# Layer 3 of a graph network: GpSimd waits for every tenth gather to land, and the edge products are planned later and further apart

## The chip, the cores and the metric

One core of one Trainium2 chip runs the whole program in one launch. The metric is the device time of that launch in microseconds (us). The kernel before takes 5139.83 us, the median of three runs that lie between 5138.98 and 5140.54. The profile is one more execution, which took 5172.93 us with the profiler on; its instructions span 5171.2 us of that.

## The reference, cut to what matters

Four layers of a graph network are applied one after another to 6250 nodes with 128 features and 100,000 directed edges, sorted by destination. Only the last one, layer 3, is touched. It is ten steps of a propagation (APPNP):

```
src, dst = edges plus one loop for each node
norm     = 1/sqrt(deg[src]) * 1/sqrt(deg[dst])
xk = h
for step in range(10):
    agg = segment_sum(norm[:, None] * xk[src], dst)      # for each node, over its edges
    xk  = 0.9 * agg + 0.1 * h
out = x + relu(xk)
```

Each step needs the whole result of the step before it.

## The kernel before, in words

The nodes lie in 49 tiles of 128. In layer 3 the sum over edges is done in two ways.

**Dense part.** For the destination tiles 0 to 39 (`DENSE` = 40) the kernel has built a dense matrix of edge counts in fp8, which is read from HBM again in every step. TensorE takes these tiles in ten chunks of four. A chunk is 49 source tiles times 2 matmuls (a high and a low fp16 half of the node values), 98 matmuls of 128x512, all into one PSUM bank (line 1952). ScalarE copies the bank out (line 1438), TensorE turns it back with four transposes (line 1964), and VectorE combines it with the residual (line 2849); ScalarE (line 1429) and VectorE (line 2827) make the two fp16 halves for the next step.

**Edge part.** For the other nine tiles, 40 to 48 (the "pooled" tiles), the sum goes over edges. Their edges fill 145 tiles of 128. GpSimd gathers the 128 source rows of each with an indirect DMA from HBM (line 1003), from `table` in one step and from `x_spill` in the next. VectorE makes a one-hot matrix of destinations (line 2837, "hots"), and TensorE multiplies the two (line 1982). Four edge tiles are one group (`EG`), so a step has 37 groups, the last of one tile. The gathered rows go to a ring of five groups (`ERING`): GpSimd waits on `edge_used` until the group five before has been multiplied. The one-hots have a ring of four (`EHOT`). Before a step's first gather GpSimd waits on `y_out`, which counts the stores of the whole result of the step before to HBM (SyncE, line 762).

**The order.** Every engine of layer 3 goes through one and the same list, `plan`. An entry has a due time in units of one dense matmul. A step is `LONG` = 980 units (10 chunks of 98). A chunk's copy is due at its end, its turn ten units later (`TURN_LAG`) and its store 26 units later (`STORE_LAG`), so those of the last chunk fall into the next step. The products of edge group g are due at `EDGE_LAG + EDGE_GAP * g` = 64 + 20 g units of their step, the last group at 784; the one-hots of a group come 50 units ahead of it. A pooled tile is finished with its last group, and its store comes 16 units later. The sort puts these entries between the dense matmuls; the engines then run their lists in order and wait on semaphores, so TensorE stands still if a group's rows have not landed. SyncE's list holds the stores and the loads of the dense matrix. GpSimd does not follow the plan: it runs through the gathers as fast as the rings let it.

`tiles_done(step, i)` gives the number of finished node tiles, in the plan's order, up to tile i of a step. In step 1 and later, the dense matmuls of chunk 0 wait at source tiles 0, 32, 36 and 48 until the step before has finished what they read (`READ_UPTO`).

Of the kernel before, what the change touches and what calls it, by code (L numbers as in the profile page):

```python
# [15 lines left out]
P = 128  # L16
N_NODES, N_EDGES, D = 6250, 100000, 128
# [27 lines left out]
AS_KEPT_FIRST = 4  # L45
ADJ_PITCH = 1 << 13
CHUNKS = (DENSE + CHUNK - 1) // CHUNK
TURN_LAG, STORE_LAG, EDGE_LAG, EDGE_GAP = 10, 26, 64, 20
SCALE = 1024.0

BD, BK = 5, 26
# [37 lines left out]
def build(nc, t, out):  # L89
    ctx = ExitStack()  # L90
    with ctx:
# [262 lines left out]
            return (near_last[i] - edge_first) // EG  # L354

        LONG = chunk_at_cost(CHUNKS)
        finished = [(chunk_at_cost(c + 1) + TURN_LAG, list(chunk_nodes(c))) for c in range(CHUNKS)]
        finished += [(EDGE_LAG + EDGE_GAP * pooled_group(i), [i]) for i in range(DENSE, NT)]
        done_order = [i for _, some in sorted(finished) for i in some]
        place = {i: p for p, i in enumerate(done_order)}  # L360
        STORES = CHUNKS + POOLED

        plan = []
        for step in range(STEPS):
            base = step * LONG
            for c in range(CHUNKS):
                for i in range(NT):
                    plan.append((base + chunk_at_cost(c) + 2 * i * len(chunk_nodes(c)) / CHUNK, 0, "dense", step, c, i))
                plan.append((base + chunk_at_cost(c + 1), -1, "copy", step, c, 0))
                plan.append((base + chunk_at_cost(c + 1) + TURN_LAG, 1, "turn", step, c, 0))  # L370
                plan.append((base + chunk_at_cost(c + 1) + STORE_LAG, 4, "store", step, c * CHUNK, chunk_nodes(c).stop))
            for g in range(EGROUPS):
                plan.append((base + EDGE_LAG + EDGE_GAP * g, 2, "edges", step, g, 0))
                plan.append((base + EDGE_LAG + EDGE_GAP * g - 5 * EDGE_GAP // 2, 5, "hots", step, g, 0))
            for i in range(DENSE, NT):
                plan.append((base + EDGE_LAG + EDGE_GAP * pooled_group(i), 3, "pooled", step, i, 0))
                plan.append((base + EDGE_LAG + EDGE_GAP * pooled_group(i) + STORE_LAG - TURN_LAG, 4, "store", step, i, i + 1))
        plan = [entry[2:] for entry in sorted(plan, key=lambda entry: entry[:2])]

        def tiles_done(step, i):  # L380
            return step * NT + place[i] + 1

        READ_UPTO = {0: 32, 32: 36, 36: NT - 1, NT - 1: NT}

# [464 lines left out]
        def _(pool):  # L849
# [141 lines left out]
            def after_l2(b):  # L991
                if b == 0:
                    pool.sem_inc(sem("edge_used"), ERING - AS_KEPT_FIRST)
                    def two_steps(pairs):
                        for half in range(2):
                            pool.wait_ge(sem(f"y_out{half}"), pairs * (16 * STORES) + (16 * STORES if half else 16 * PTN))
                            settle(pool)
                            for g in range(EGROUPS):
                                pool.wait_ge(sem("edge_used"), pairs * (2 * EGROUPS) + (half * EGROUPS + g + 1))
                                settle(pool)  # L1000
                                for k in range(group_size(g)):
                                    tile = edge_first + g * EG + k
                                    pool.indirect_dma_start(  # L1003
                                        out=y_rows[:, g % ERING, k, :], out_offset=None, in_=(table, x_spill)[half],
                                        in_offset=bass.IndirectOffsetOnAxis(ap=src_i[:, tile:tile + 1], axis=0)
                                    ).then_inc(y_in[g % ERING], 16)

                    for pairs in range(STEPS // 2 - 1):
                        two_steps(pairs)
                    two_steps(STEPS // 2 - 1)  # L1010
                if b:
                    with pool.Fori(0, STEPS) as s:
                        pool.wait_ge(sem("y_stored"), s * 16 + 16)
                        settle(pool)
                        sweep(s + 3, table, src_i)
                        wait_runs(s + 4)
                        node_rows(runs, nodes(Db), sem("nodes3"))
# [503 lines left out]
        def _(pe):  # L1521
# [363 lines left out]
            def after_l2(b):  # L1885
# [46 lines left out]
                if b == 0:  # L1932
# [4 lines left out]
                    for kind, step, what, i in plan:  # L1937
                        n = step * CHUNKS + what
                        if kind == "dense":
                            some, y = chunk_nodes(what), halves((E, A)[step % 2])  # L1940
                            r = [i < last for _, last in PARTS3].index(True)
                            piece, at = n * len(PARTS3) + r, (i - PARTS3[r][0]) * P
                            if i == PARTS3[r][0]:
                                pe.wait_ge(sem(f"adj_in{piece % ADJ_RING}"), 16 * (piece // ADJ_RING + 1))
                            if i == 0 and n >= 2:
                                pe.wait_ge(sem("turn_in"), n - 1)
                            if n == 0 and i % T7 == 0:
                                pe.wait_ge(sem("y_lower0"), i // T7 + 1)
                            if n > 0 and what == 0 and i in READ_UPTO:
                                pe.wait_ge(sem("lower"), max(tiles_done(step, j) for j in range(READ_UPTO[i])))  # L1950
                            for h in range(2):
                                mm = pe.matmul(chunk_banks[n % 2][:, 0:len(some) * P], y[:, i, h * D:(h + 1) * D],  # L1952
                                               adj_ring[:, piece % ADJ_RING, 0:len(some), at:at + P],
                                               start=(i == 0 and h == 0), stop=(i == NT - 1 and h == 1))
                            if i == NT - 1:
                                mm.then_inc(sem("chunk_made"), 1)
                            elif i + 1 == PARTS3[r][1]:
                                mm.then_inc(sem("piece_used"), 1)
# [8 lines left out]
                        if kind == "edges":  # L1967
                            g, r = what, what % ERING
                            pe.wait_ge(y_in[r], step * row_loads[r] + y_in_before[r]
                                       + 16 * sum(group_size(q) for q in range(r, g + 1, ERING)))  # L1970
                            pe.wait_ge(sem("edge_hot_made"), step * EGROUPS + g + 1)
                            for k in range(group_size(g)):
                                tile = edge_first + g * EG + k
                                of = [i for i in near(tile) if i >= DENSE]
                                for i in of:
                                    first = max(near_first[i], edge_first)
                                    if tile == first:
                                        if i - 2 >= DENSE:
                                            tiles_free(step, i - 2)
                                        else:  # L1980
                                            tiles_free(step - 1, max(range(DENSE + (i - DENSE) % 2, NT, 2)))
                                    mm = pe.matmul(edge_banks[i % 2][:, 0:2 * D], step_hot[g % EHOT][:, k, i % 2 * P:(i % 2 + 1) * P],  # L1982
                                                   y_rows[:, r, k, :].bitcast(F16),
                                                   start=(tile == first), stop=(tile == near_last[i]))
                                    if tile == near_last[i]:
                                        mm.then_inc(sem("multiplied"), 1)
                            if g < EGROUPS - 1:
                                mm.then_inc(sem("edge_used"), 1)
# [77 lines left out]
        def _(dve):  # L2066
# [658 lines left out]
            def after_l2(b):  # L2725
# [81 lines left out]
                if b == 0:  # L2807
# [22 lines left out]
                    for kind, step, what, _ in plan:  # L2830
                        if kind == "hots":
                            g, nth = what, step * EGROUPS + what
                            if nth >= EHOT:
                                dve.wait_ge(sem("edge_used"), ERING + nth - EHOT + 1)
                            for k in range(group_size(g)):
                                at = edge_first + g * EG + k
                                a = dve.tensor_scalar(step_hot[g % EHOT][:, k, :], iota_y, dst_f[:, at:at + 1], UNIT,
                                                      ALU.is_equal, MUL)
                            a.then_inc(sem("edge_hot_made"), 1)
                        if kind == "turn":  # L2840
# [217 lines left out]
```

## Time and profile before

| what | value |
| --- | --- |
| median of 3 runs | 5139.83 us |
| profiled execution | 5172.93 us |
| its span | 5171.2 us |
| PE busy in the span | 4366.7 us, 84% |
| GpSimd (POOL) busy | 3123.1 us, 60% |
| layer 3, first to last dense matmul start | 2726.2 to 5160.7 us |
| gathers of layer 3 (line 1003) | 1450, mean 954 ns |
| idle time of GpSimd before them | 588.3 + 516.2 us |

Layer 3 is the second half of the span, about 2435 us in ten steps. In the 40 slices of the profile the digits of PE are all 9 there, and those of GpSimd are 4 to 7. The profiled execution is some 33 us longer than the median of the unprofiled ones.

### The profile page before, as it was taken

What the parts mean: (1) busy time and instruction counts of PE and PEld (TensorE: products, weight loads), DVE (VectorE), ACT (ScalarE), POOL (GpSimd) and SP (SyncE); (2) the same over time, 40 slices, a digit from 0 to 9 for tenths busy, and PEclk for the clock granted to TensorE, in tenths of its full rate; (3) what the DMA queues carried; (4) which work ended last, traced back from release to release, by engine and by line L of the source; (5) the groups of instructions that cost most, each with busy time, mean ns of one, the idle gap of its engine ahead of it and who ended that gap; (6) DMA issues with size and microseconds to landing.
All of it is one profiled execution on the core that took longest, in us unless ns stands there. A gap on an engine that the chain in (4) does not pass through costs nothing.

```text
span 5171.2 us, 68624 instructions
## 1 busy us (share of the span) xinstructions
PE 4366.7 (84%) x24174; PEld 2788.4 (54%) x24174; DVE 2619.2 (51%) x8500; ACT 1031.3 (20%) x2920; POOL 3123.1 (60%) x3205
## 2 busy tenths in 40 slices
PE   3798589999984556566668999999999999999999
PEld 3676466666664555555544444444454545454444
DVE  7898545665554677777884222323232323222232
ACT  5787411111111011112241000000000000000001
POOL 2554277777776777777725564747474747465564
PEclk9999789999996676787688999999999999999999
DMA  5322222222222333333316565656565656565564
GB/s 149 96 101 92 85 67 71 70 66 71 70 70 74 96 95 97 95 94 95 87 31 194 186 188 178 196 182 190 182 192 181 193 181 188 182 192 185 184 191 144
DMA packets 454493, 682.92 MB, mean 132 GB/s; under 512 B 89793, under 2 KB 235879, under 8 KB 454128
## 3 DMA queue, kind: packets, MB, share of 16 engines
q1 hardware_dynamic: 346116, 463.55, 28.6%
q0 software_dynamic: 101664, 211.69, 15.7%
q8 instruction: 198, 3.24, 0.3%
q10 hardware_dynamic: 6364, 3.20, 0.2%
q14 instruction: 151, 1.24, 0.1%
HBM read 595.40 MB, written 83.11 MB: 131 GB/s over the span
## 4 chain that ended last, share of the span: by engine, by line
PE 30%; POOL 18%; issue 7%; DVE 6%; DMA 4%; ACT 1%; POOLq 0%; DVEq 0%
PE ps L1952 23%; POOL arena L1003 13%; POOL E L968 5%; PE pt L1982 2%; DMA arena<-table,src_i 2%; PE ps L1774 2%; DVE B L2481 1%; DMA arena<-x_spill,src_i 1%; DVE arena L2523 1%; PE pt L1791 1%; PE pt L1782 1%; PE ps L1964 1%; DMA E<-gat_table,src_i 0%; PE ps L1901 0%; ACT C L1303 0%
## 5 line engine op out<-in xcount | busy, mean ns | idle before, releaser
L1952 PE MATMUL ps<-arena,E 128*128 128x512 fp8e4 x4900 | 1099.8, 380 | 7.0 <-DVE C L2750 7.0
L1952 PE MATMUL ps<-arena,A 128*128 128x512 fp8e4 x4900 | 1095.7, 379 | 0.0
L1003 POOL DMA_INDIRECT arena<-table,src_i x725 | 691.8, 954 | 588.3 <-DMA table<-E 368.9
L1003 POOL DMA_INDIRECT arena<-x_spill,src_i x725 | 691.5, 954 | 516.2 <-DMA x_spill<-A 296.8
L953 POOL DMA_INDIRECT arena<-table,src_i x782 | 741.8, 949 | 355.2 <-issue 235.9
L968 POOL DMA_INDIRECT E<-gat_table,src_i x782 | 762.5, 975 | 270.7 <-issue 234.1
L1697 PE MATMUL ps<-E,arena 128*128 128x352 f32 (+22 forms) x2932 | 740.5, 404 | 113.8 <-DMA arena<-table,src_i 112.8
L1952 PEld LDWEIGHTS ps<-arena,E 128*128 128x128 f16 x4900 | 480.5, 98 | 539.6 <-DVE C L2750 7.2
L1952 PEld LDWEIGHTS ps<-arena,A 128*128 128x128 f16 x4900 | 479.4, 98 | 529.1
L1697 PEld LDWEIGHTS ps<-E,arena 128*128 128x128 f32 x2932 | 493.5, 202 | 287.4 <-DMA arena<-table,src_i 136.0
L2849 DVE SCALAR_TENSOR_TENSOR C<-ps,sc_b,scores 128x128 f32<-128x128 f32 x400 | 112.6, 344 | 821.7 <-PE ps L1964 820.6
L2401 DVE SCALAR_TENSOR_TENSOR E<-arena,pt 128x512 f32<-128x512 bf16 (+5 forms) x782 | 478.5, 674 | 24.7 <-PE ps L1697 23.9
L1774 PE MATMUL ps<-arena,B 128*128 128x144 f32 x2244 | 475.1, 362 | 0.0
L1774 PEld LDWEIGHTS ps<-arena,B 128*128 128x128 f32 x2244 | 389.5, 239 | 8.1 <-issue 6.0
L1038 POOL DMA_INDIRECT A<-first_rows,src_i x145 | 213.5, 1472 | 210.6 <-PE pt L2020 117.2
L2862 DVE SCALAR_TENSOR_TENSOR scores<-pt,sc_b,scores 128x128 f32<-128x128 f32 x90 | 31.6, 351 | 597.4 <-PE pt L1982 597.0
L1822 PE MATMUL pt<-ident,E 128*128 128x128 f32 x56 | 25.3, 452 | 360.3 <-ACT E L1237 360.3
L1507 ACT ACTIVATE E<-ps 128x490 fp8e4<-128x490 f32 (+1 forms) x520 | 307.2, 596 | 92.2 <-PE ps L2036 88.2
L2045 PE MATMUL pt<-arena,E 128*128 128x258 f16 x1960 | 305.0, 276 | 1.0 <-ACT E L1507 1.0
L1438 ACT ACTIVATE O<-ps 128x512 f32<-128x512 f32 x100 | 59.7, 597 | 1118.7 <-PE ps L1952 1118.4
L2977 DVE TENSOR_SCALAR O<-arena 128x245 bf16<-128x245 bf16 x1040 | 232.3, 278 | 37.4 <-PE ps L2036 37.2
L2481 DVE TENSOR_SCALAR B<-w_gat,dst_f 128x256 f32<-128x256 bf16 x784 | 245.0, 381 | 0.0
(351 smaller groups left out, 4748.5 us busy)
## 6 DMA issues: line engine op xcount, KB each, us to landing
arena<-adj SPq DMA_DIRECT2D x200, 1024.0 KB
arena<-adj SPq DMA_DIRECT2D x100, 1088.0 KB
adj<-E SPq DMA_DIRECT2D x40, 784.0 KB, 3.4
O<-dst_rows SPq DMA_DIRECT2D x112, 224.0 KB, 3.5
arena<-table,src_i POOLq DMA_INDIRECT x1507
x_spill<-A SPq DMA_DIRECT2D x50, 256.0 KB
E<-gat_table,src_i POOLq DMA_INDIRECT x782
E<-in_etype SPq DMA_DIRECT2D x781, 16.0 KB
```

The source lines that it names most:

```text
L953: pool.indirect_dma_start(out=rows_ring[:, k % RING, :], out_offset=None, in_=table, in_offset=bass.IndirectOffsetOnAxis(ap=src_i[:, k:k + ...
L968: pool.indirect_dma_start(out=att_rows[:, b % 3 * AB + at, :], out_offset=None, in_=gat_table, in_offset=bass.IndirectOffsetOnAxis(ap=src_ ...
L1003: pool.indirect_dma_start(out=y_rows[:, g % ERING, k, :], out_offset=None, in_=(table, x_spill)[half], in_offset=bass.IndirectOffsetOnAxis ...
L1038: pool.indirect_dma_start(out=rows0[:, x % (2 * EG0), :], out_offset=None, in_=first_rows, in_offset=bass.IndirectOffsetOnAxis(ap=src_i[:, ...
L1507: act.activation(made[:, i % MADE, :, 2 * BD * q:2 * BD * q + w], ps[pair % 4][:, 0:w * NT].rearrange("p (d j) -> p j d", j=NT), ACT.Copy, ...
L1697: mm = pe.matmul(ps[m % 4][:, (lo - WD * m) * BASES:(hi - WD * m) * BASES], rows_ring[:, k % RING, :], m_ring[:, k % MS, lo - first_dst(k) ...
L1774: mm = pe.matmul(ps[i % 2][:, 0:WL2], edge_hot[:, (2 * b + half) % 3, k % AH, i % 2 * P:(i % 2 + 1) * P], weighted_rows[:, b % 2, k, :], s ...
L1952: mm = pe.matmul(chunk_banks[n % 2][:, 0:len(some) * P], y[:, i, h * D:(h + 1) * D], adj_ring[:, piece % ADJ_RING, 0:len(some), at:at + P] ...
L2045: mm = pe.matmul(bank0_of(m)[:, 0:2 * LO], made[:, m % MADE, j, :], y16[:, j, :], start=(j == 0), stop=(j == NT - 1))
L2401: dve.scalar_tensor_tensor(m_ring[:, k % MS, w, :], bc(iota_h[:, w], BASES), dst_rel[:, k:k + 1], row_bc(made_c[:, c % 2, at, :], w.stop - ...
L2481: a = dve.tensor_scalar(edge_hot[:, g % 3, k, :], iota_y, dst_f[:, g * AH + k:g * AH + k + 1], None, ALU.is_equal)
L2977: dve.tensor_scalar(hot_code[:, g % HOT, 0:BW], iota_w[:, 0:BW], slot_c[:, g // P, g % P:g % P + 1], None, ALU.is_equal).then_inc(sem("hot ...
```

## The change

GpSimd gets a wait behind every tenth gather of a step, counted from the step's start (14 waits in the 145 gathers of a step): until that gather has landed. The edge groups are planned at 84 + 25 g instead of 64 + 20 g units of a step, and at 148 + 25 g in the first step. With this the last group is due at 984 units, four units into the next step, and in the first step at 1048, 68 units into the second. As tiles of one step now finish while the next one runs, the finishing order is read off the plan for all steps at once instead of being computed for one step, and the ring of one-hots is counted through all steps, not anew in each.

```diff
-TURN_LAG, STORE_LAG, EDGE_LAG, EDGE_GAP = 10, 26, 64, 20
+TURN_LAG, STORE_LAG, EDGE_LAG, EDGE_LATE, EDGE_GAP = 10, 26, 84, 148, 25
...
-        finished = [(chunk_at_cost(c + 1) + TURN_LAG, list(chunk_nodes(c))) for c in range(CHUNKS)]
-        finished += [(EDGE_LAG + EDGE_GAP * pooled_group(i), [i]) for i in range(DENSE, NT)]
-        done_order = [i for _, some in sorted(finished) for i in some]
-        place = {i: p for p, i in enumerate(done_order)}
...
+            first = base + (EDGE_LAG if step else EDGE_LATE)
             for g in range(EGROUPS):
-                plan.append((base + EDGE_LAG + EDGE_GAP * g, 2, "edges", step, g, 0))
-                plan.append((base + EDGE_LAG + EDGE_GAP * g - 5 * EDGE_GAP // 2, 5, "hots", step, g, 0))
+                plan.append((first + EDGE_GAP * g, 2, "edges", step, g, 0))
+                plan.append((first + EDGE_GAP * g - 5 * EDGE_GAP // 2, 5, "hots", step, g, 0))
...
+        done = [(step, i) for kind, step, what, _ in plan if kind in ("turn", "pooled")
+                for i in (chunk_nodes(what) if kind == "turn" else [what])]
+        place = {of: p for p, of in enumerate(done)}
...
         def tiles_done(step, i):
-            return step * NT + place[i] + 1
+            return place[step, i] + 1
...
                                     ).then_inc(y_in[g % ERING], 16)
+                                    if (g * EG + k) % 10 == 10 - 1:
+                                        pool.wait_ge(y_in[g % ERING], y_in_before[g % ERING]
+                                                     + (2 * pairs + half) * row_loads[g % ERING] + 16 * (k + 1)
+                                                     + 16 * sum(group_size(q) for q in range(g % ERING, g, ERING)))
...
-                                    mm = pe.matmul(edge_banks[i % 2][:, 0:2 * D], step_hot[g % EHOT][:, k, ...],
+                                    mm = pe.matmul(edge_banks[i % 2][:, 0:2 * D], step_hot[(step * EGROUPS + g) % EHOT][:, k, ...],
```

## Rows read from the trace of the kernel before

**Rows 1.** The head of the page: the span, and TensorE's busy time in it.
```profile
span 5171.2 us, 68624 instructions
PE 4366.7 (84%) x24174; PEld 2788.4 (54%) x24174; DVE 2619.2 (51%) x8500; ACT 1031.3 (20%) x2920; POOL 3123.1 (60%) x3205
```

**Rows 2.** Waits of TensorE in layer 3: us in total, times, longest.
```profile
PE pt L1982 <- DMA arena<-table,src_i: 33.4, 28, 15.6
PE pt L1982 <- DMA arena<-x_spill,src_i: 19.8, 25, 1.7
```

**Rows 3.** Stretches: length, PE busy (instructions), granted clock, DMA share, GB/s.
```profile
2726.00:2987.00 261.00, 241.50 (x1205) 0.96 0.60 189
2987.00:3229.50 242.50, 237.40 (x1211) 1.00 0.59 186
```

**Rows 4.** The dense line: durations in ns, first and last start in us.
```profile
L1952 PE MATMUL ps<-arena,E x4900: 378/379/634, 2726.2 to 4919.9; 128*128 128x512 fp8e4 x196
L1952 PE MATMUL ps<-arena,A x4900: 379/379/380, 2987.1 to 5160.7; 128*128 128x512 fp8e4 x196
```

**Rows 5.** Pieces of the chain of waits: start, us, what.
```profile
2902.93 7.05 DMA arena<-table,src_i
...
2947.16 21.15 PE ps L1952 x98
...
3237.23 0.73 issue
...
3306.57 0.44 PE ps L1964 x4
...
3317.17 0.44 PE pt L1982 x4
```

**Rows 6.** Timeline, third step: start, us, engine, line [idle before <-releaser].
```profile
3237.96 0.94 POOL L1003 DMA_INDIRECT arena<-table,src_i  x1 [60.32 <-DMA table<-E]
...
3244.23 0.61 PE L1982 MATMUL pt<-arena,rows 128*128 128x256 f16 x4
...
3250.21 0.61 PE L1982 MATMUL pt<-arena,rows 128*128 128x256 f16 x4 [1.06 <-DMA arena<-table,src_i]
...
3260.72 0.61 PE L1982 MATMUL pt<-arena,weight_e 128*128 128x256 f16 x4 [0.40 <-DMA arena<-table,src_i]
...
3276.12 0.61 PE L1982 MATMUL pt<-arena,rel_i 128*128 128x256 f16 x4 [0.31 <-DMA arena<-table,src_i]
...
3418.76 0.95 POOL L1003 DMA_INDIRECT arena<-table,src_i  x1 [0.30 <-issue]
```

**Rows 7.** Timeline, first step, its first gather and first edge group.
```profile
2726.18 17.30 PE L1952 MATMUL ps<-arena,E 128*128 128x512 fp8e4 x66 [7.00 <-DVE C L2750]
...
2752.80 0.94 POOL L1003 DMA_INDIRECT arena<-table,src_i  x1 [130.41 <-DMA table<-E]
...
2759.04 1.04 PE L1982 MATMUL pt<-arena,rows 128*128 128x256 f16 x4 [15.57 <-DMA arena<-table,src_i]
2759.87 5.91 PE L1952 MATMUL ps<-arena,E 128*128 128x512 fp8e4 x20
```

**Rows 8.** Stretch behind the 7 us idle time, columns as in Rows 3.
```profile
2726.00:2731.00 5.00, 4.82 (x12) 0.50 1.04 392
```

**Rows 9.** Timeline: end of a step's pooled work, and a last chunk's store.
```profile
3234.78 0.36 SPq L762 DMA_DIRECT2D table<-E  x1
...
3427.26 0.27 PE L1982 MATMUL pt<-arena,rows 128*128 128x256 f16 x1
...
3429.10 3.45 SPq L762 DMA_DIRECT2D x_spill<-A  x2
...
3432.08 1.13 DVE L2817 SCALAR_TENSOR_TENSOR scores<-C,sc_a,B 128x128 f32<-128x128 f32 x4
```

**Rows 10.** Timeline, the end of the last step.
```profile
5162.52 1.12 DVE L2849 SCALAR_TENSOR_TENSOR C<-ps,sc_b,scores 128x128 f32<-128x128 f32 x4 [16.87 <-PE ps L1964]
```

**Rows 11.** DMA of the third step, 3189 to 3430 us: packets, MB, share.
```profile
q0 software_dynamic: 4640, 9.51, 13.9%
```

More of the change, by code:

```diff
@@ L371, in build @@
                 plan.append((base + chunk_at_cost(c + 1) + STORE_LAG, 4, "store", step, c * CHUNK, chunk_nodes(c).stop))
+            first = base + (EDGE_LAG if step else EDGE_LATE)
             for g in range(EGROUPS):
-                plan.append((base + EDGE_LAG + EDGE_GAP * g, 2, "edges", step, g, 0))
-                plan.append((base + EDGE_LAG + EDGE_GAP * g - 5 * EDGE_GAP // 2, 5, "hots", step, g, 0))
+                plan.append((first + EDGE_GAP * g, 2, "edges", step, g, 0))
+                plan.append((first + EDGE_GAP * g - 5 * EDGE_GAP // 2, 5, "hots", step, g, 0))
             for i in range(DENSE, NT):
-                plan.append((base + EDGE_LAG + EDGE_GAP * pooled_group(i), 3, "pooled", step, i, 0))
-                plan.append((base + EDGE_LAG + EDGE_GAP * pooled_group(i) + STORE_LAG - TURN_LAG, 4, "store", step, i, i + 1))
+                plan.append((first + EDGE_GAP * pooled_group(i), 3, "pooled", step, i, 0))
+                plan.append((first + EDGE_GAP * pooled_group(i) + STORE_LAG - TURN_LAG, 4, "store", step, i, i + 1))
         plan = [entry[2:] for entry in sorted(plan, key=lambda entry: entry[:2])]
+        done = [(step, i) for kind, step, what, _ in plan if kind in ("turn", "pooled")
+                for i in (chunk_nodes(what) if kind == "turn" else [what])]
+        assert [step for step, _ in done] == [step for step in range(STEPS) for _ in range(NT)]
+        place = {of: p for p, of in enumerate(done)}
         def tiles_done(step, i):
-            return step * NT + place[i] + 1
+            return place[step, i] + 1
         READ_UPTO = {0: 32, 32: 36, 36: NT - 1, NT - 1: NT}
@@ L1949, in after_l2 @@
                             if n > 0 and what == 0 and i in READ_UPTO:
-                                pe.wait_ge(sem("lower"), max(tiles_done(step, j) for j in range(READ_UPTO[i])))
+                                pe.wait_ge(sem("lower"), max(NT + tiles_done(step - 1, j) for j in range(READ_UPTO[i])))
                             for h in range(2):
@@ L1981, in after_l2 @@
                                             tiles_free(step - 1, max(range(DENSE + (i - DENSE) % 2, NT, 2)))
-                                    mm = pe.matmul(edge_banks[i % 2][:, 0:2 * D], step_hot[g % EHOT][:, k, i % 2 * P:(i % 2 + 1) * P],
+                                    mm = pe.matmul(edge_banks[i % 2][:, 0:2 * D], step_hot[(step * EGROUPS + g) % EHOT][:, k, i % 2 * P:(i % 2 + 1) * P],
                                                    y_rows[:, r, k, :].bitcast(F16),
@@ L2836, in after_l2 @@
                                 at = edge_first + g * EG + k
-                                a = dve.tensor_scalar(step_hot[g % EHOT][:, k, :], iota_y, dst_f[:, at:at + 1], UNIT,
+                                a = dve.tensor_scalar(step_hot[nth % EHOT][:, k, :], iota_y, dst_f[:, at:at + 1], UNIT,
                                                       ALU.is_equal, MUL)
```

## The prediction

> **What bounds the kernel now.** I read the head of the page first: the span is 5171.2 us and PE is busy for 84% of it [rows 1]. The dense line of layer 3 starts at 2726.2 us and its last matmul at 5160.7 us [rows 4], so the ten steps take 2434.7 us; nothing ahead of them is touched. The stretches of the first two steps, cut at the first dense matmul of each, are 261 and 242.5 us long with PE busy for all but a few us in the second [rows 3]. Steps 2 to 10 together are (5160.9 - 2987.1), which is 241.5 us each [rows 4]. The bound is TensorE, and what it waits for inside layer 3 is the landing of gathers: 33.4 us and 19.8 us, of which one wait is 15.6 us [rows 2].
>
> What would a step take without waits? In the chain 98 dense matmuls take 21.15 us, 215.8 ns each, a chunk's four transposes 0.44 us, four edge matmuls 0.44 us [rows 5]. The second step has 1211 matmuls [rows 3], 980 dense, 40 transposes, and about 189 of edges. So 980 x 0.2158 = 211.5, plus 10 x 0.44 = 4.4, plus 189 x 0.11 = 20.6: **236.5 us**. A later step loses 241.5 - 236.5 = 5.0 us, nine of them 45 us. This is more than the waits say (37.6 us), since a wait also costs the drain and refill around it; I take the difference of lengths. The first step loses 24.4 us. Of these about 4.3 belong to its start: 66 dense matmuls took 17.30 us [rows 7] instead of 14.2, behind a 7 us idle time, and some waiting for the state. The other 20.1 are the edges: 15.57 us of waiting for the first group and, behind it, 20 dense matmuls in 5.91 us [rows 7] instead of 4.48. So **65 us hang on late gathers**, and this is all that the change can win.
>
> Why are they late? In the third step GpSimd issues its first gather at 3237.96 and its 145th at 3418.76 [rows 6]: 180.8 us over 144 gaps, 1.256 us a gather, 5.02 us for four. TensorE asks for a group every 20 units: 20 x 0.2158 + 20.6/37 + a share of the transposes 0.09 = 4.96 us. The two have the same pace, the gathers a little slower. TensorE reaches its first group just when it lands and then has no lead, so that each gather with a longer latency stops it.
>
> **The new plan.** At 25 units a group TensorE asks every 25 x 0.2158 + 0.56 + 0.11 = 6.06 us, and its first group comes 20 units = 4.3 us later. Without the new wait GpSimd would gain a us on every group and soon be held by the ring of five. No stall of a step would be left except at its start. The number of edge matmuls is unchanged.
>
> **The new wait.** The profile before has no such wait; the price is worked out from landings. Gather n of the third step starts at 3237.96 + 1.256 n. The first group's last gather (n = 3) starts at 3241.7 and TensorE goes on at 3244.23: 2.5 us. The other groups of the first eight for which it waited give 3.5 (n = 7, 3250.21), 4.0 (n = 15, 3260.72) and 4.4 us (n = 27, 3276.12) [rows 6]; the four without a wait landed sooner than asked for. The longest piece of the chain from a gather's issue to its landing that I use is 7.05 us [rows 5]. TensorE meets the late ones, so a typical landing is nearer to the first two: 3.4 us. GpSimd then resumes; behind the y_out wait this took 0.73 us [rows 5], with more than one wait in it; I take 0.4. A wait puts off the next gather, which would have come 1.256 us after the tenth, by 3.4 + 0.4 - 1.26 = **2.6 us** (bounds: 1.3 from the fastest landing and an instant restart, 6.5 from the longest and 0.73). 14 waits are 36 us a step, and GpSimd's pace becomes 5.02 + 36/36.25 = 6.0 us a group, again the same as TensorE's 6.06. Behind the waiting instruction stand only the next gathers; their cover is the lead.
>
> How long is the cover? The step of rows 6 began at 3229.5 [rows 3], so its gathers started 8.5 us into it. In the changed kernel VectorE does the last pooled tile first, about 0.8 us in the way of the last chunk, which makes it 9.3. The last gather then lands at 9.3 + 180.8 + 36 + 3.4 = 229.5; TensorE wants the last group at 236.5 + 4 units = 237.4. The slack is 8 us, or 0.55 us for each wait. **A wait may cost 3.15 us before a step becomes longer.** At the start the lead is 84 x 0.2158 + 0.44 = 18.6 against a first landing at 9.3 + 3.8 + 2.5 to 3.5, two to three us. I leave 3 us in all for single late landings in the eight later steps.
>
> The Trainium skill ("DMA: Bandwidth & Descriptors", section "Anatomy of one DMA — SWDGE (gpsimd) path") fits a DMA as 2.0 us plus its bytes over 436 GB/s. A gather here is 9.51 MB/145 = 66 KB [rows 11], so it says 2.15 us, an estimate from that page. The fastest landing read above is 2.5 us and the others up to 4.4, so the trace is above the rule; by it a wait would cost 1.3 us and the sum below would be some 4 us better.
>
> **The first two steps.** The first gather of layer 3 starts at 2752.80 [rows 7], set by the stores ahead of it, 26.6 us into the step. Group 0 is now wanted at 148 units, 31.9 + 0.4 + the slow start 3.1 = 35.4 us, 2761.6; it landed at 2759.04. The 15.57 us and the slower stretch behind them go. They are partly paid in the second step: the last group of the first is due 68 units into it, 14.7 + 0.44 + 1.0 = 16.1 us. From such a last group to its store are 3429.10 - 3427.26 = 1.84 us, and from a store to the first gather 3237.96 - 3234.78 = 3.18 us [rows 6, 9]. So gathers start at 21.1 us, group 0 lands at 21.1 + 3.8 + 3 = 27.9, and TensorE wants it at 18.1 + 0.44 + 1.0 = 19.6: a stall of **8.3 us**. Behind 7 us of idle time the clock was 0.50, the 1.2 GHz level, for 5 us [rows 8], twelve matmuls where 23 fit: I add **3 us**. From there the pace is even, and the third step starts as usual.
>
> Chunk 0 of the second step reads tile 48 at unit 96, 28 units (6 us) behind the last group; 1.84 us are enough. SyncE's stores move with their tiles; the ones past which a step's gathers wait is the last chunk's (unit 1006), behind tile 48's (unit 1000), in all steps but the first.
>
> **The end.** Group 36, its VectorE work of some 1.5 us and four residual operations of 1.13 us [rows 9] now stand ahead of the last chunk's, which began 1.6 us behind the last dense matmul [rows 4, 10]: about **1.5 us**.
>
> **Sum.** 65 - 8.3 - 3 - 3 - 1.5 = 49 us. The profiled execution would go from 5172.9 to 5124. Profiled and unprofiled differ by 33 us of which I cannot place any, so I take the same 49 us off the median: 5139.8 - 49 = **5091 us**.
>
> **Rivals.** *A wait of no weight.* If landings are near the 2.5 us row, or the restart instant, the 3 us and a us of the second step's stall go: 5086. For it speaks the first group; against it the three longer ones.
>
> *The gathers become the pace.* If a wait costs 3.3 us, in the middle between mine and the rows of late landings, nine steps grow by 14 x (3.3 - 3.15) + about a us for uneven landings, 3 us each: 5118. For it: the two paces, 6.0 and 6.06, are a tie.
>
> *The gathers overrun the step (the other side).* The place is GpSimd's queue: each us over 3.15 a wait costs 14 us a step, 140 in all, so from 3.5 us a wait (a mean landing of 4.35 with my restart) the gain is gone. At a mean landing of 5 us, as the chain's longer pieces, a wait costs 4.15: 140 us more, 5231. For it: the dense matrix is loaded beside the gathers at 186 GB/s [rows 3], and landings of 7.05 us exist. Against it: 317 of 370 groups were never waited for (53 waits [rows 2]) though GpSimd was no faster than TensorE.
>
> *The late plan reaches over each step's end.* If the gathers started late in every step, as in the second, this would cost 8 to 11 us ten times, some 90 us: 5180. Against it: unit 1000 comes ahead of 1006.
>
> **Chances.** The forecast 0.62, no weight 0.07, the gathers as pace 0.18, overrun 0.09, every step late 0.04. A change of 0.2% (10 us) can be told from none. Faster by more: the first three less a tail of the third, 0.85; the same 0.04; slower 0.11. The likeliest case alone is 5080 to 5105. For eight in ten the low end is the case in which only the second step's stall is left, 5139.8 - 65 = 5075, and the high end lies past the third case, 5128.
>
> **What will show it.** TensorE's waits for gathers fall from 53 us to 10 to 15, most of them one wait at the second step's first group. Steps 3 to 10 are 236.5 to 237.5 us; the second about 248. GpSimd has 14 waits a step on its own gathers, and its gathers stretch from 181 to about 217 us. Steps of 240 us and more with gathers on the chain to the end would mean the third or fourth case, and a first gather more than 12 us into each step the fifth.

## The result, and the profile after

The changed kernel takes 5154.07 us (median of 20 runs), the kernel before 5140.18 us (20 runs beside them): ratio **1.0027**, 95% interval 1.002 to 1.0035. It is slower by a quarter of a per cent, where 49 us less were forecast.

The profiled execution seems to say the opposite: its span is 5148.8 us against 5171.2 [rows 1].

```profile
span 5148.8 us, 68624 instructions
PE 4371.8 (85%) x24174; PEld 2791.6 (54%) x24174; DVE 2618.0 (51%) x8500; ACT 1032.6 (20%) x2920; POOL 3081.0 (60%) x3205
```

The dense line, with first and last start, tells why:

```profile
L1958 PE MATMUL ps<-arena,E x4900: 379/379/634, 2690.9 to 4894.6; 128*128 128x512 fp8e4 x196
L1958 PE MATMUL ps<-arena,A x4900: 379/379/634, 2935.5 to 5137.2; 128*128 128x512 fp8e4 x196
```

Layer 3 begins at 2690.9 us instead of 2726.2 [rows 4]: the layers ahead of it, in which nothing was changed, took 35 us less in this execution. In two later executions on another chip it began at 2735.7 (kernel before) and 2737.3 us (changed), so this start varies between executions. Inside layer 3, from the first dense matmul to the end of the last, the kernel before took 2434.7 us and the changed one 5137.4 - 2690.9 = 2446.5 us: **12 us more**, close to the 14 us of the timed runs. Only layer 3's own length is compared below.

By step (length, PE busy, granted clock, DMA share, GB/s; steps 1 to 4 and 10):

```profile
2690.90:2935.50 244.60, 238.52 (x1197) 0.99 0.62 199
2935.50:3194.20 258.70, 243.11 (x1219) 0.97 0.56 176
3194.20:3437.50 243.30, 238.53 (x1210) 0.99 0.59 185
3437.50:3680.30 242.80, 238.21 (x1210) 0.99 0.59 186
4894.80:5137.40 242.60, 238.52 (x1210) 0.99 0.55 173
```

Against [rows 3] and 241.5 us for a later step: the first step became 16 us shorter, the second 16 longer, and the eight others are 242.9 us each on average instead of 241.4, 1.5 more, which makes the 12. Forecast were 236.5 to 237.5 for these eight.

What TensorE and GpSimd waited for (us in total, times, longest):

```profile
PE pt L1988 <- DMA arena<-x_spill,src_i: 33.5, 14, 8.0
PE pt L1988 <- DMA arena<-table,src_i: 22.7, 10, 4.0
```
```profile
POOL arena L1005 <- DMA arena<-table,src_i: 208.8, 68, 4.9
POOL arena L1005 <- DMA arena<-x_spill,src_i: 202.3, 65, 4.7
POOL arena L1005 <- PE pt L1988: 28.6, 15, 7.0
```

TensorE has 24 waits for gathers instead of 53 [rows 2], but they sum to 56.2 us instead of 53.2: few and long ones. GpSimd stands 3.1 us at a time before the gather behind a wait, of which 0.3 is the usual gap (133 of the 140 waits; the other seven ended later, with the ring or an issue gap). From the start of a gather with a wait behind it to the next gather's start 4.1 us pass on average, where 1.25 are usual: **2.9 us a wait**. The source view of the gathers gives landings, of the 280 gathers (of 1450) for which it can tell them; it gave none before:

```profile
DMA to landing us min/median/max: 2.4/3.4/5.6
```

One later step of GpSimd, and the place at which TensorE stops (timeline of the fourth step):

```profile
3446.80 1.84 POOL L1005 DMA_INDIRECT arena<-x_spill,src_i  x1 [20.05 <-DMA x_spill<-A]
...
3458.95 0.95 POOL L1005 DMA_INDIRECT arena<-x_spill,src_i  x1 [0.30 <-issue]
3462.16 0.94 POOL L1005 DMA_INDIRECT arena<-x_spill,src_i  x1 [2.26 <-DMA arena<-x_spill,src_i]
...
3613.90 0.95 POOL L1005 DMA_INDIRECT arena<-x_spill,src_i  x1 [0.30 <-issue]
...
3619.17 0.94 POOL L1005 DMA_INDIRECT arena<-x_spill,src_i  x1 [4.32 <-DMA arena<-x_spill,src_i]
3620.37 0.36 SPq L736 DMA_DIRECT2D arena<-adj  x1
3620.41 0.94 POOL L1005 DMA_INDIRECT arena<-x_spill,src_i  x1 [0.30 <-issue]
...
3625.78 1.04 PE L1988 MATMUL pt<-arena,rel_i 128*128 128x256 f16 x4 [3.72 <-DMA arena<-x_spill,src_i]
3626.61 3.73 PE L1958 MATMUL ps<-arena,A 128*128 128x512 fp8e4 x12
...
3669.25 0.94 POOL L1005 DMA_INDIRECT arena<-x_spill,src_i  x1 [0.31 <-issue]
```

The gathers start 9.3 us into the step and spread over 222.4 us, from 3446.80 to 3669.25, instead of 180.8 [rows 6]. That is 41.6 us for 14 waits, 3.0 us each with a few gaps of another kind in it. The wait behind the gather of 3613.90 is the eleventh of the step, behind gather 110 (counted from one). It costs 4 us; the next gathers run beside a load of the dense matrix that SyncE issues at 3620.37, and the one of 3620.41 lands some 5.3 us after its issue. Group 27 (gathers 109 to 112) needs it, and TensorE stands for 3.72 us. Behind the stall twelve dense matmuls take 3.73 us where 2.75 are usual: another us. A stall of 3.6 to 4.0 us stands at this place in each of the eight later steps. The waits of TensorE in this step are 4.6 us (0.9 of them at group 21); with the slow stretch they explain 5.6 of the 6.3 us over 236.5. The last group starts 12.4 us after its gather's issue: there is slack at the step's end.

### The profile page after: what moved, and what is told of

Read it like the earlier page. It is cut to its first block, busy times and chain, and to the rows that moved or that the text cites. A ratio compares the mean times of both kernels' runs of the same rounds, so it can differ in the third digit from the quotient of the medians.

```text
span 5148.8 us, 68624 instructions
## 1 busy us (share of the span) xinstructions
PE 4371.8 (85%) x24174; PEld 2791.6 (54%) x24174; DVE 2618.0 (51%) x8500; ACT 1032.6 (20%) x2920; POOL 3081.0 (60%) x3205
## 4 chain that ended last, share of the span: by engine, by line
PE 23%; POOL 15%; issue 9%; DVE 6%; DMA 4%; ACT 1%; POOLq 0%; DVEq 0%
PE ps L1958 18%; POOL arena L1005 14%; DMA arena<-x_spill,src_i 2%; DMA arena<-table,src_i 2%; PE pt L1988 2%; PE ps L1780 1%; DVE B L2487 1%; POOL E L970 1%; DVE arena L2529 1%; PE pt L1788 1%; PE pt L1797 1%; PE ps L1907 0%; PE ps L1970 0%; ACT C L1309 0%; DVE arena L2510 0%
## 5 line engine op out<-in xcount | busy, mean ns | idle before, releaser
L1044 POOL DMA_INDIRECT A<-first_rows,src_i x145 | 152.3, 1051 | 235.2 <-PE pt L2026 142.9
L2843 DVE TENSOR_SCALAR rows<-w_gat,dst_f 128x256 f16<-128x256 bf16 x726 | 160.0, 292 | 213.4 <-PE pt L1988 213.2
```

The source lines that it names most:

```text
L2843: a = dve.tensor_scalar(step_hot[nth % EHOT][:, k, :], iota_y, dst_f[:, at:at + 1], UNIT, ALU.is_equal, MUL)
```

## Experiments

The experiments ran in five batches, each on another chip: the kernel before took 6340 us (median) in the first, 5171 in the second, and 6357, 6366 and 6344 in the last three. Kernels are compared only with the kernel before in the same batch. I call the chip of the second the one like the result's, the others the slow chips.

**The plan alone**: the changed kernel without its waits.

```diff
-                                    if (g * EG + k) % 10 == 10 - 1:
-                                        pool.wait_ge(y_in[g % ERING], ...)
```

> The changed kernel without its 14 waits a step; the plan (84 + 25 g, 148 + 25 g in the first step) stays. Theory (the waits cost what the plan gave): gathers of a step stretch over 181 us instead of 222, TensorE's stalls of about 5 us in the middle of steps 3 to 10 go, and these steps take 236.5 to 237.5 us instead of 243. The second step keeps a stall of about 8 us at its first group and takes 248 to 252 us instead of 259; the first 240 to 242. In all some 60 to 70 us less than the changed kernel: 5085 to 5097. Rival (the plan itself costs: last group past the step's end, work of the pooled tile ahead of the last chunk): 5145 or more, steps 3 to 10 at 240 us and above.

On a slow chip: 6006.3 us against 6340.0, ratio 0.947 (0.945 to 0.948). Neither number could be set against the forecast, so it was run again together with the changed kernel:

> The changed kernel without its waits, as before. If this chip is as the one of the result: 5085 to 5097 us, ratio 0.990, steps 3 to 10 of 237 us. On a chip as that of the first experiments 6006 again, ratio 0.947.

> The changed kernel, unchanged. If this chip is as the one of the result: 5154 us, ratio 1.0027. On a chip as that of the first experiments (plan alone 6006, wait alone 6244, before 6340): the theory that a wait costs time to landing puts it between the plan alone and every 20th gather's step of 257 us plus as much again, steps of 260 to 264 us, 6080 to 6120 us, 4% faster than before. Rival (the waits help on such a chip, as the wait alone beats the kernel before there): under 6000.

On the chip like the result's: plan alone 5108.7 us, ratio **0.9885** (0.985 to 0.992); the changed kernel 5187.6 us, ratio **1.0041** (1.002 to 1.006); the kernel before 5170.7 us. The steps of the plan alone (columns as above):

```profile
2727.40:2966.80 239.40, 238.19 (x1197) 0.99 0.65 205
2966.80:3214.60 247.80, 239.85 (x1218) 0.98 0.59 182
3214.60:3451.10 236.50, 236.50 (x1210) 1.00 0.61 190
3451.10:3687.60 236.50, 236.50 (x1210) 1.00 0.61 190
4870.20:5106.70 236.50, 236.50 (x1210) 1.00 0.57 177
```

A later step is 236.5 us, with no idle time of TensorE at all. In all of layer 3 TensorE waits once for a gather, at the second step's first group, and GpSimd is now held by the ring of five instead:

```profile
PE pt L1984 <- DMA arena<-x_spill,src_i: 8.0, 1, 8.0
```
```profile
POOL arena L1005 <- PE pt L1984: 218.9, 203, 1.8
```

So the plan gives what was forecast of it, and the 14 waits a step take back all of it: between the two kernels lie 79 us on this chip, in the traces (5193.9 - 2737.3) - (5106.7 - 2727.4) = 77 us. The rival, a cost of the plan itself at the step's end, is refuted: that would have left steps of 240 us and more.

The kernel before on the same chip:

> The kernel before, unchanged, for its profile on the chip of these runs. On the chip of the first experiments it took 6340 us, against 5140 where the change was timed. [...] If this chip is as the one of the result: 5140 and steps of 241.5 us.

5184.0 us in its one run, layer 3 in 5172.5 - 2735.7 = 2436.8 us, as in the first trace. The plan alone is 57.5 us shorter there, the changed kernel 19.8 us longer.

**Waits for what has long landed**: the 14 waits stay, each for group g - 2.

```diff
-                                        pool.wait_ge(y_in[g % ERING], ... + 16 * (k + 1) + 16 * sum(... q in range(g % ERING, g, ERING)))
+                                        pool.wait_ge(y_in[(g - 2) % ERING], ... + 16 * sum(... q in range((g - 2) % ERING, g - 1, ERING)))
```

> The changed kernel with its 14 waits in place, but each for the landing of the group two before, which is long down: the instruction stays and the landing time goes. Theory (it is the time to landing, 3.4 us, and not the wait instruction): within 5 us of the plan alone, gathers of a step over 181 to 185 us. Rival (the wait instruction itself breaks GpSimd's run of gathers, 1 us or more each): 195 us and more for the gathers of a step, yet TensorE's steps would still be 237.

On the slow chip 6000.6 us, ratio 0.947 (0.945 to 0.949), the same as the plan alone beside it. GpSimd has gaps of its own on that chip, so the gathers of a step stretch over 216 to 220 us with either kernel and not over the 181 to 185 expected. The gap at a wait can be read all the same. Here are the tenth and the eleventh gather of the fourth step:

```profile
4239.99 0.95 POOL L1005 DMA_INDIRECT arena<-x_spill,src_i  x1 [0.30 <-issue]
4241.24 0.94 POOL L1005 DMA_INDIRECT arena<-x_spill,src_i  x1 [0.30 <-issue]
```

They start 1.25 us apart, which is the median over all 140 such places of the trace and over all other pairs as well; in the changed kernel the same two gathers stand 3.21 us apart (3458.95 and 3462.16 above). So the wait instruction costs nothing. What separates the changed kernel from the plan alone on the chip like the result's, 79 us, is then the time to landing, and the trace puts GpSimd's idle time down to it.

**Half as many waits**:

```diff
-                                    if (g * EG + k) % 10 == 10 - 1:
+                                    if (g * EG + k) % 20 == 20 - 1:
```

> The changed kernel with a wait behind every twentieth gather, 7 a step. Theory (a pace: 5.02 + 7 x 2.94/36.25 = 5.59 us a group against TensorE's 6.06, with a lead of 2 to 3 us): the gathers take 202 us a step, stalls in steps 3 to 10 nearly vanish, 237 to 238 us each: 5088 to 5102, within 8 us of the plan alone. Rival (each wait costs TensorE its own share): halfway between the changed kernel and the plan alone, about 5120.

> A wait behind every twentieth gather, 7 a step, as before, now on a chip like that of the result. Theory: steps 3 to 10 at 236.5 us as with the plan alone, the ratio to the kernel before 0.988 to 0.991. Rival (each wait costs TensorE a share): steps of 240 us, ratio 0.995 to 0.997. If the chip is like that of the first experiments, 0.956 again.

Both fell on slow chips: 6059.0 us, 0.9561 (0.954 to 0.959), and 6070.0 us, 0.9558 (0.952 to 0.959). Beside the plan alone of the first batch (0.947) this is 53 us more. The forecast of 8 us at most is missed. It does not fail at the gathers, though: in both traces TensorE waits for a gather once, 8.2 and 8.3 us at the second step's first group, as with the plan alone. The later steps are 257.7 and 259.0 us long against 253.2 with the plan alone, and what lengthens them stays open. What seven waits cost on a chip like the result's was not measured.

**The waits alone**, in the kernel before:

```diff
                                     ).then_inc(y_in[g % ERING], 16)
+                                    if (g * EG + k) % 10 == 10 - 1:
+                                        pool.wait_ge(y_in[g % ERING], ...)
```

> The kernel before with the 14 waits alone, at 64 + 20 g. Theory: the gathers of a step need 222 us and TensorE wants a group every 4.96 us; the last gather lands at 8.5 + 222 + 3.4 = 234 us of a step, the last group was due at 177, and about 42 us of other work follow it, so a step takes some 276 us: 34 to 36 us more in each of ten, 5480 to 5500. Rival (GpSimd's waits are covered by the ring of five): under 5200.

> The kernel before with the 14 waits alone, at 64 + 20 g. On a chip like that of the result, with the waits at 2.9 us each: the gathers take 222 us a step and the last group, due at 177 us, is ready at 234; with the 42 us of work behind it a step is some 276 us: 35 us more in each of ten, ratio 1.065 to 1.072, 5480 to 5530.

On slow chips again: 6243.6 us, 0.985 (0.983 to 0.987), and 6318.8 us, 0.993 (0.989 to 0.996). Layer 3 took 6231.2 - 3439.7 = 2791.5 us in the first trace, 279 us a step, near the 276 that the pace gives, but 2854.8 us in the second, 285 a step; and the kernel before is slower still on such a chip, which I had not foreseen. The expected total is missed, and there is no answer for a chip like the result's.

**Eleven waits**, without the last three or without the first three of a step:

```diff
+ if (g * EG + k) % 10 == 10 - 1 and g * EG + k < 110:      # without the last three
+ if (g * EG + k) % 10 == 10 - 1 and g * EG + k > 30:       # without the first three
```

> The changed kernel without the last three of a step's 14 waits (behind gathers 120, 130 and 140). Theory (TensorE and the gathers meet in the middle: by gather 110, eleven waits have put the gathers off by 33 us, and group 27 is the one stall of a later step, 3.8 us; what comes behind it is covered): the stall stays, steps 3 to 10 still 241.5 to 243.5 us, the time within 8 us of the changed kernel's. Rival (the bound is the step's end, as the forecast's slack had it): 8 us a step less for the gathers, steps of 237 us, 55 us faster than the changed kernel.

> The changed kernel without the first three waits (behind gathers 10, 20 and 30), eleven again. Theory: at group 27 the gathers are 7 us less behind, which is more than the stalls at groups 21 and 27 together (5 us), so steps 3 to 10 take 236.5 to 237.5 us and the second loses its small stalls behind the first: 55 to 65 us faster than the changed kernel, near the plan alone. Rival (the number of waits counts, not the place): the same as without the last three.

> The changed kernel without the last three waits of a step, once more. On a chip like that of the result: theory (the stall is in the middle, at group 27, behind eleven waits): steps 3 to 10 still at 241 to 243.5 us with one stall of 3 to 4 us at group 27, ratio 1.001 to 1.005 to the kernel before. Rival (the step's end binds): steps of 237 us, ratio 0.990.

> The changed kernel without the first three waits, once more. On a chip like that of the result: theory: no stall at group 27, steps 3 to 10 of 236.5 to 237.5 us, ratio 0.988 to 0.991. Rival (the number of waits counts and not the place, or the end binds as well): as without the last three, within 5 us.

> The changed kernel without the last three waits of a step, third try for a chip like that of the result. Theory there (the waits bind at group 27): steps 3 to 10 of 241 to 243.5 us, ratio 1.001 to 1.005. Rival (they bind at the step's end): steps of 237 us, ratio 0.990. On a chip on which the kernel before takes 6340 us the two can't be told apart: ratio 0.952 to 0.957.

> The changed kernel without the first three waits, third try. Theory on a chip like that of the result: no stall at group 27, steps of 236.5 to 237.5 us, ratio 0.988 to 0.991. Rival (the number of waits counts, or the end binds): within 5 us of the kernel without the last three. On the other kind of chip 0.952 to 0.957.

All six runs fell on slow chips. Without the last three: 0.957, 0.952, 0.9585. Without the first three: 0.954, 0.9515, 0.959, with intervals of 0.004 to 0.006 on either side. No difference, and on these chips none was to be expected: TensorE's idle time there is mostly in issue gaps. Inconclusive. The traces point the way of the theory, but by few us: without the first three waits TensorE waits for one gather only, that at the second step's first group (8.1, 8.1 and 7.8 us), and without the last three for 4, 7 and 2 gathers (11.2, 17.1 and 8.8 us). That the waits bind at group 27 and not at the step's end is read from the traces of the changed kernel (its second one on the chip like the result's has the same stall, 3.6 to 4.1 us, in all eight later steps) and was not shown by an experiment.

**The two kernels on a slow chip**, for their traces:

> The changed kernel for its profile. On a chip like that of the result: one stall of 3.8 us at group 27 of each later step, 5150 to 5200 us. On a chip on which the kernel before takes 6340 us: 6080 to 6130 us, steps of 262 us.

> The kernel before for its profile. On a chip like that of the result: steps of 241.5 us. On a chip on which it takes 6340 us: steps of 285 us, of which TensorE waits 15 us for gathers and 30 us in issue gaps; GpSimd's own gaps, not landings, stretch the gathers to over 210 us a step (there the plan alone had 217).

The changed kernel took 6039.2 us in one run, the kernel before 6344.3. Layer 3 took 6025.9 - 3494.0 = 2531.9 us in the changed kernel, 6333.0 - 3455.4 = 2877.6 in the kernel before. In the latter GpSimd has 80 gaps before gathers that the trace gives to no work of this core, and TensorE waits most for ScalarE's copy of a bank:

```profile
PE ps L1964 <- ACT O L1438: 199.7, 30, 20.6
PE ps L1952 <- issue: 94.9, 116, 2.4
```
```profile
POOL arena L1003 <- remote: 225.2, 80, 5.5
POOL arena L1003 <- PE pt L1982: 98.5, 55, 5.7
```

In the changed kernel the first of these rows is:

```profile
PE ps L1970 <- ACT O L1444: 18.1, 10, 4.2
```

With these 225 us of gaps and some of other kinds the gathers of a step stretch over 209 to 217 us in the kernel before instead of 181, some 5.9 us a group against the 4.96 at which the old plan asks; the new plan asks every 6.06 or later. That this is why the new plan wins there is argued, not shown. Shown is that the change took 5% off on such a chip in its one run (6039.2 against 6365.5 us, the batch's median before), and that the plan alone, with 0.947, has all of it. In these single traces the waits cost nothing there: layer 3 took 5999.6 - 3451.5 = 2548 us with the plan alone, in another batch, and a later step is 253 us in both. With seven and eleven waits it was 2555 to 2607 us, on four chips, so the time does not follow the number of waits on slow chips, and these runs say nothing on what a wait costs on the other kind.

**Without waits, and a first step that ends in time**:

```diff
-TURN_LAG, STORE_LAG, EDGE_LAG, EDGE_LATE, EDGE_GAP = 10, 26, 84, 148, 25
+TURN_LAG, STORE_LAG, EDGE_LAG, EDGE_LATE, EDGE_GAP = 10, 26, 84, 132, 24
```

> No waits, edge groups at 84 + 24 g and at 132 + 24 g in the first step, so that the first step's last group (unit 996) and its store (1012) come near the last chunk's (1006). Theory: the stall of 8 to 10 us at the second step's first group goes, about 2 us appear in the first step (group 0 wanted at 31.5 us, landed at 33), 8 to 12 us less than the plan alone. Rival (the 16 units less of lead or the tighter gap cost more): the same as the plan alone or slower.

```profile
2710.50:2955.00 244.50, 240.92 (x1205) 0.98 0.64 201
2955.00:3194.00 239.00, 236.95 (x1211) 1.00 0.61 189
```

The first step's last group is due at unit 996 instead of 1048. These are the first two steps, columns as above. The second step is 239.0 us instead of 247.8, the first 244.5 instead of 239.4, and layer 3 5086.1 - 2710.5 = 2375.6 us, 3.7 us less than with the plan alone and not the 8 to 12 expected. The timed ratio is 0.991 (0.988 to 0.994), not to be told from 0.9885. Both beat the kernel before and the changed one.

## Why the prediction was wrong

**The 65 us that hang on late gathers: right.** The plan alone gives 57.5 us of them in layer 3, and its later steps are the 236.5 us worked out from 980, 40 and 189 matmuls.

**The first two steps: right in kind, too small in size.** The stall at the second step's first group was put at 8.3 us and is 8.05. The slow stretch behind it was put at 3 us; 24 dense matmuls take 6.30 us instead of 5.34 (7.26 with the plan alone), so it is one to two. The first step lost its 15.6 us wait. But the pace was to be even from there, and with the waits both steps stall again: the first 244.6 instead of 239.4 us, the second 258.7 instead of 247.8.

**The end: right.** VectorE reaches the last chunk 1.4 us later, counted from the last dense matmul, of 1.5 forecast.

**What a wait costs: 2.6 us forecast, 2.9 to 3.0 measured.** The landing was right, 3.4 us in the median of the 280 that the trace tells. But the waits meet the loads of the dense matrix more often than other gathers do: the DMA engines were over 60% busy with other transfers in the 3.4 us behind 47% of the gathers with a wait, and behind 39% of the others. Such gathers land later (last section).

**"A wait may cost 3.15 us before a step becomes longer": this is the step that failed.** It set the gathers' last landing against TensorE's last group, 8 us of slack, and took an even pace in between. At 3.0 us a wait it would still have held. But the last group is the one with most room: it has a single tile, so its gather comes three gathers, 3.8 us, sooner than that of a full group. The same sum at group 27 gives, in the prediction's own terms, a landing at 9.3 + 111 x 1.256 + 11 x 2.6 + 3.4 = 180.7 us and a group wanted at 18.6 + 27 x 6.06 = 182.2: 1.5 us of slack, or 0.14 for each of its eleven waits. It gives 1.5 to 2.1 us at every other full group, too. And the pace was not the forecast 6.0 against 6.06 but 5.02 + 41.6/36.25 = 6.17. Eleven of the 14 waits come before group 27 is complete, in three quarters of the step, so by then the gathers are (11 x 3.0) - 27 x (6.06 - 5.02) = 5 us further behind than at the start, the lead is gone, and a landing of 5.3 us meets it. The slack at the end is there and useless: what TensorE has lost at group 27 does not come back. The 3 us put down for late landings in all eight steps together were 6.4 us in each on average (3.8 to 8.0), 51 us; with 5 and 11 us in the first two steps this is the 49 us that were forecast, and more.

**The rival that came true** is "the gathers become the pace", in place and kind; it was priced at 3 us a step, from 0.15 us a wait over a limit that did not exist in this form, and had a chance of 0.18. Its condition, 3.3 us a wait, was not met; 2.9 to 3.0 were enough, and its real price is twice that. Of what should show it, "steps of 240 us and more with gathers on the chain" is what came.

The sum by the measured terms: the plan alone takes 55 us (against the first trace, 2434.7 - 2379.3) or 57.5 us (same chip) off layer 3; the waits put 67 or 77 us back, which leaves 12 or 20 us more.

On a slow chip the same change was 5% faster in its one run. No view of the one profile before showed a slow chip, and nothing in the forecast speaks to it.

## What to carry to other kernels

Two queues that feed each other at the same pace need their slack reckoned at every point, not at the end: write down who is ahead after each wait and take the worst point. Here that was 1.5 us at group 27 and at others like it, not the 8 of the last group. A wait for a transfer just issued costs the queue that transfer's whole time to landing, less the one gap that would have passed anyway, and more where other transfers are in flight. Where the kernel before has been slowed by the layers ahead of the change in its one profile, compare the stage, not the span.

## What the runs showed of the hardware

The same kernel took 5140 us, 5171 us and 6340 to 6366 us in different batches. On the slow ones TensorE and GpSimd have gaps of up to 8 us for which the trace has no releaser on this core, and layer 3 begins at 3440 to 3494 us instead of 2691 to 2737. What the gaps are stays open, as does why the waits alone made the kernel before 0.7 to 1.5% faster there.

An idle time of 3.7 us of TensorE was followed by dense matmuls at less than full pace (twelve in 3.73 us instead of 2.75), one of 8 us by 24 in 6.30 us instead of 5.34. The granted clock fell with it: in part of the 5 us behind each it was at the 1.2 GHz level (0.50), and then full again. These are those 5 us and the next 5 (length, PE busy, granted clock, DMA share, GB/s):

```profile
3625.80:3630.80 5.00, 5.00 (x19) 0.72 0.20 52
3630.80:3635.80 5.00, 5.00 (x28) 1.00 0.40 103
2963.70:2968.70 5.00, 5.00 (x20) 0.73 0.23 56
2968.70:2973.70 5.00, 5.00 (x29) 1.00 0.80 251
```

Gathers land 2.4 to 5.6 us after issue, and the later the more else is in flight. Of the 280 landings, 80 had the DMA engines less than 20% busy with other transfers in the 3.4 us behind the issue, and their median is 2.5 us; 105 had them over 60% busy, and theirs is 4.4. No run changed this traffic, so that it is the cause is argued from the one trace. The Trainium skill ("DMA: Bandwidth & Descriptors", section "Anatomy of one DMA — SWDGE (gpsimd) path") would give 2.15 us for 66 KB as an estimate; the trace has a median of 3.4, and comes near the page's figure only with little else in flight (2.5). By the rule a wait costs 1.3 us, and eleven of them would have been covered at group 27. The measurement decides.
